# Gate and token transposes moved behind the next logits, tanh ahead of the normalisation, and beta's additions in half-size pieces

## The reference

```python
x = x + _L0_conv_ref(_gn(x), ...)     # temporal and spatial attention, graph convolution, layer norm
x = x + _L1_conv_ref(_gn(x), ...)     # mixture of experts: 8 experts, the best 2 for each position
```

```python
lhs = jnp.einsum('bnft,n->btf', x, U1) @ U2
rhs = jnp.einsum('f,bnft->bnt', U3, x)
E = jnp.einsum('kj,bij->bik', V_e, jax.nn.sigmoid(jnp.einsum('btn,bns->bts', lhs, rhs) + b_e))
x_tat = jnp.einsum('bnfj,bjt->bnft', x, _col_softmax(E))
lhs2 = jnp.einsum('bnft,t->bnf', x_tat, W1) @ W2
rhs2 = jnp.einsum('f,bnft->btn', W3, x_tat)
S = jnp.einsum('kj,bij->bik', V_s, jax.nn.sigmoid(jnp.einsum('bnt,btm->bnm', lhs2, rhs2) + b_s))
S = _col_softmax(S)
for k in range(3):
    r = jnp.einsum('mn,bmn,bmft->bnft', cheb[k], S, x)
    out = out + jnp.einsum('bnft,fo->bnot', r, Theta[k])
y = relu(rw * x + rb + conv_1x3(relu(out)) + tb)
return (y - mean(y)) / sqrt(var(y) + 1e-5) * gamma + beta      # over the last axis, 16 long
```

## Time and profile before

| what | us |
|---|---|
| median of 3 runs | 689.44 (686.73 to 690.37) |
| the profiled execution | 687.6 |
| its span | 685.8 |
| TensorE busy | 538.0 (78%) |
| VectorE busy | 395.7 (58%) |
| ScalarE busy | 253.8 (37%) |
| GpSimd busy | 198.6 (29%) |

### The profile page before, as it was taken

One profiled execution on the slowest core, in us unless ns is written; L12 is line 12 of the kernel. 1 busy time (PEld: TensorE's weight loads), 2 busy tenths in 40 slices (PEclk: granted clock), 3 DMA queues, 4 the chain that ended last, 5 costly groups with the idle time before them and its releaser, 6 DMA issues.

```text
span 685.8 us, 11952 instructions
## 1 busy us (share of the span) xinstructions
PE 538.0 (78%) x2664; PEld 363.6 (53%) x2665; DVE 395.7 (58%) x1697; ACT 253.8 (37%) x619; POOL 198.6 (29%) x267
## 2 busy tenths in 40 slices
PE   0557279989999999999983309999999999999243
PEld 0223147767776677676762204666666666665122
DVE  4745123788888888888899652333333333332265
ACT  0435833443444444444432201333333333333232
POOL 5000000113333333333334430434433433434000
PEclk9989558999999999999996557999999999999555
DMA  9900000000000000000010141222222222221697
GB/s 304 423 7 2 0 1 0 1 1 25 32 34 30 32 32 32 32 34 30 32 39 32 39 132 55 85 78 88 84 83 87 84 84 90 84 84 35 206 298 231
DMA packets 36260, 52.86 MB, mean 77 GB/s; under 512 B 4605, under 2 KB 31360, under 8 KB 35968
## 3 DMA queue, kind: packets, MB, share of 16 engines
q1 hardware_dynamic: 24816, 30.86, 14.3%
q0 software_dynamic: 6480, 16.85, 6.6%
q10 hardware_dynamic: 4928, 4.72, 2.1%
HBM read 30.19 MB, written 23.14 MB: 78 GB/s over the span
## 4 chain that ended last, share of the span: by engine, by line
PE 47%; DVE 31%; DMA 8%; issue 7%; ACT 4%; SPq 1%; POOL 1%; DVEq 0%; POOLq 0%; ACTq 0%
PE bank L614 18%; PE bank L629 9%; DMA xT<-yrows 5%; DVE vq L1012 4%; PE bank L492 4%; PE bank L601 2%; PE bank L622 2%; DVE vq L1011 2%; PE bank L377 2%; DVE work L1173 2%; PE bank L459 2%; DVE work L1189 2%; ACT xs L714 2%; DVE work L1224 1%; PE bank L367 1%
## 5 line engine op out<-in xcount | busy, mean ns | idle before, releaser
L614 PE MATMUL bank<-w,xT 128*128 x284 | 137.5, 607 | 2.0 <-DVE xT L1413 2.0
L1413 DVE COPY xT<-bank 128x256 f32<-128x256 f32 x71 | 30.2, 425 | 145.8 <-PE bank L601 145.8
L978 POOL DMA_INDIRECT yrows<-xT,dest x71 | 69.6, 980 | 141.1 <-ACT xT L834 137.0
L492 PE MATMUL bank<-work 128*128 128x256 f32 x384 | 95.0, 391 | 0.0
L946 POOL DMA_INDIRECT xrows<-xtok,slot x64 | 67.2, 1050 | 92.2 <-DVEq L1310 75.1
L492 PEld LDWEIGHTS bank<-work 128*128 128x128 f32 x384 | 71.9, 194 | 9.6 <-issue 0.8
L629 PE MATMUL bank<-w,xT 128*128 x284 | 73.3, 380 | 1.6 <-ACT xT L839 1.6
L935 POOL TENSOR_TENSOR yg<-work,sml 128x512 f32<-128x512 f32 x16 | 17.9, 1121 | 191.2 <-DVE work L1224 191.2
L614 PEld LDWEIGHTS bank<-w,xT 128*128 128x128 f32 x284 | 49.4, 194 | 38.1 <-issue 38.1
L828 ACT ACTIVATE xT<-bank 128x256 f32<-128x256 f32 x71 | 27.3, 384 | 97.4 <-PE bank L614 97.4
L629 PEld LDWEIGHTS bank<-w,xT 128*128 128x128 f32 x284 | 48.5, 190 | 6.2 <-issue 2.6
(11 more groups left out here) (200 smaller groups left out, 993.2 us busy)
## 6 DMA issues: line engine op xcount, KB each, us to landing
xT<-xrows SPq DMA_DIRECT2D x71, 129.0 KB
xT<-yrows SPq DMA_DIRECT2D x32, 256.0 KB, 3.9
xs<-x_in SPq DMA_DIRECT2D x4, 1024.0 KB, 10.2
w<-w13t_in SPq DMA_DIRECT2D x1, 4096.0 KB, 18.4
out<-xT ACTq DMA_DIRECT2D x16, 256.0 KB, 4.1
w<-w2t_in SPq DMA_DIRECT2D x1, 2048.0 KB, 22.8
yrows<-xT,dest POOLq DMA_INDIRECT x71, 2.4
xrows<-xtok,slot POOLq DMA_INDIRECT x64
```

Of the source, the lines that this page charges most:

```text
L492: last = mm(bank[6][:, h * N:(h + 1) * N], z[:, p, c, k, h], A[:, p, c, k], start=(c == 0 and k == 0), stop=(c == C - 1 and k == K - 1))
L614: last = mm(bank[2 + q][:, :], xc[:, q, c], w13[:, e, c].rearrange("p w n -> p (w n)"), start=(c == 0), stop=(c == C - 1))
L978: pool.indirect_dma_start(yrows, bass.IndirectOffsetOnAxis(ap=dest[:, q], axis=0), yo[:, q], None, bounds_check=2 * TOKENS - 1, oob_is_err ...
L1413: V.tensor_copy(xc[:, q].rearrange("p c k -> p (c k)"), bank[q][:, 0:C * P]).then_inc(c_xc, 1)
```

## The change

There are three edits. In the turn of the middle stage TensorE does `tokens` and `turn_logits` of an image one turn later, behind the logits and around the first part of the graph; ScalarE copies them at the start of that turn. ScalarE does `tanh` and the second `copy_features` ahead of `normalise`. On VectorE `route_a` is no longer woven with the statistics; it begins the chain that `route_b` continues. In the first stage `add_beta` takes a group: 16 pieces of 128x256 for each of the two, group 0's two by two behind the copies of group 1's images, and group 1's as 7, 1 and 8 around the second tanh and exp.

```diff
             def turn(i, q, ahead2, ahead1, now, back1, back2, back3):      # TensorE
                 if ahead1:
                     logits(i + 1, 1 - q)
+                if back3:
+                    tokens(i - 3, 1 - q)
                 if now:
                     graph(i, q, 0, 0)
+                if back3:
+                    turn_logits(i - 3, 1 - q)
+                if now:
                     graph(i, q, 0, 1)
...
                 if back3:
                     prefix(i - 3, 1 - q)
-                if back2:
-                    tokens(i - 2, q)
-                if back2:
-                    turn_logits(i - 2, q)
...
                     if j >= 2:
                         copy_x(g, j - 2)
+                    if g and j < GB:
+                        add_beta(0, 2 * j, 2 * j + 2)
...
-            def add_beta(first, end):
+            def add_beta(g, first, end):
 
-                act.wait_ge(a_xnv, B)
-                act.wait_ge(a_xna, B)
+                act.wait_ge(a_xnv, GB * (g + 1))
+                act.wait_ge(a_xna, GB * (g + 1))
                 for t in range(first, end):
-                    nc.scalar.activation(x_all[:, :, :, t], x_all[:, :, :, t], ACT.Identity,
+                    nc.scalar.activation(x_all[:, g, :, :, t], x_all[:, g, :, :, t], ACT.Identity,
...
-            add_beta(0, T // 2)
+            add_beta(1, 0, 7)
             temporal_tanh(1)
-            add_beta(T // 2, 3 * T // 4)
+            add_beta(1, 7, 8)
             temporal_exp(1)
-            add_beta(3 * T // 4, T)
+            add_beta(1, 8, T)
...
             def turn(i, q, ahead2, ahead1, now, back1, back2, back3):      # ScalarE
+                if back3:
+                    copy_tokens(i - 3, 1 - q)
                 if back1:
                     square(i - 1, 1 - q)
...
-                if back2:
-                    normalise(i - 2, q)
                 if ahead2:
                     tanh(i + 2, q)
                 if ahead1:
                     copy_features(i + 1, 1 - q, 1)
                 if back2:
-                    copy_tokens(i - 2, q)
+                    normalise(i - 2, q)
...
-            pool.wait_ge(x_beta, T)
+            pool.wait_ge(x_beta, GROUPS * T)
...
-                choice = router(route_b)
+                def choose():
+                    yield from router(route_a)
+                    yield from router(route_b)
+
+                choice = choose()
                 weave(centre())
-                weave(router(route_a), statistics())
+                weave(statistics())
                 variance = layer_norm()
                 weave(attention(), along=(variance, choice))
```

2 lines of the change are left out of this document (1 added, 1 removed).

## The result

| | median | range |
|---|---|---|
| kernel before, 4 runs | 688.53 us | 686.73 to 690.37 |
| changed kernel, 4 runs | 680.14 us | 677.81 to 684.61 |

The ratio is 0.9888 (95% interval 0.9853 to 0.9923): 7.7 us faster by the ratio, 8.4 by the medians. So the gain is some 8 to 10 us, with intervals of 2 us on either side. Among all the executions three were far slower than the rest (703 and 789 us of the kernel before, 1143 us of r2) and are left out. I had forecast 685.4, 4.0 us of gain, in a range from 681.2. The gain is about double, and the time outside the range.

A forecast was written before the change was run, and what follows sets the result against it. VectorE was taken to bound the middle stage, so removed TensorE or ScalarE waits count only where VectorE waits behind them. Gains of 2.0 + 1.7 + 0.3 + 0 = 4.0 us off 689.4 gave 685.4, range 681.2 to 690.5.

The forecast's parts named there:

- 682.9: Rival, chance 0.20: clock holds in the first stage and beta's pieces are at their lower bound, 2.5 us more gained.
- part 2: Router's first part on VectorE in steady turns: 0.18 us a turn, between 0.17 lost and 0.19 won.
- part 4: Last turns of the middle stage: 0.3 us gained once, bounds 0 and 3 x 0.31.
- three signs of being wrong: Steady turn not shorter, second exp moved by over 2.5 us, or square starting later behind L1198 than before.
- TensorE's waits: Gate and token transposes in steady turns: nothing gained, 0; bounds 0 and one 0.59 us copy a turn.
- The router's order: VectorE in eleven steady turns: 0.19 us won to the reciprocal, 0.01 lost behind it, 0.18 a turn, 2.0 in all.
- First turn with a router: Everything on TensorE comes 1.73 us earlier there: 1.7 us gained, bounds 0.58 and 1.73.
- The last turns: Statistics 0.31 us shorter, but tail the same chain as before: 0.3 us gained once.
- Beta: First stage: half pieces of 0.60 us on ScalarE, 1.5 us gained against 1.4 lost; 0 taken, bounds 2.5 gained, 2.3 lost.
- the clock was lost there: First stage: longer waits likely put TensorE's second eight transposes at 1.2 GHz, 1.4 us lost with the spreading matmuls.

The follow-up runs named there:

- r2: Kernel before with only beta's additions changed (half pieces, by group): 685.79 us, ratio 0.9968.
- r12: Changed kernel with ScalarE's normalisation put back ahead of tanh and the second feature copy: 688.81 us, ratio 1.0004 to the kernel before.
- r4: Kernel before with only VectorE's order changed (router's first part in one chain with the second, statistics alone): 686.12 us, ratio 0.9968.
- r6: Kernel before with only TensorE's and ScalarE's new turn orders; VectorE's order and beta as before: 686.46 us, ratio 0.9987.
- r3: Kernel before with only the three new turn orders (TensorE, ScalarE, VectorE), beta as before: 680.60 us, ratio 0.9902.
- filled pair: r13 and r15, kernel before and turns alone, both with result-neutral filler products on TensorE: 684.06 and 676.88 us.
- r13: Kernel before plus TensorE filler products that change no result, 8 at the pipeline's start and 31 ahead of the expert stage: 684.06 us, ratio 0.9948.
- r15: Kernel before with the three new turn orders only, plus the same fillers as r13: 676.88 us, ratio 0.9841.
- r1: The changed kernel unedited, run again beside the kernel before: 678.44 us, ratio 0.9849.
- r16: The whole changed kernel plus the same fillers as r13: 674.17 us, ratio 0.9817 to the kernel before.
- r14: Kernel before with beta's change only, plus the same fillers as r13: 682.01 us, ratio 0.9925.
- r17: r16 with 12 of group 0's beta pieces moved into ScalarE's wait for group 1's norm, four singly behind images 4 to 7: 669.09 us, ratio 0.9725.
- r19: r13 with 3 more fillers in front of the first image's tokens: 682.41 us, ratio 0.9916 to the kernel before.
- r7: Changed kernel with 24 filler products behind the last prefix product, ahead of the expert stage: 679.73 us, ratio 0.9865 to the kernel before.
- r9: Changed kernel with 29 filler products behind the last prefix product and 2 more ahead of the first expert product: 677.38 us, ratio 0.9832.

## Why the prediction was wrong

The time was forecast at 685.4 and came at 680.14. Of this distance 0.9 us is not the change's: I took the gain off 689.4, and the kernel before had 688.53 in the comparison. The rest is the gain, 4.0 forecast and 7.7 measured (8.4 by the medians). The range's lower end does not follow from its own terms either: 682.9 less 0.1 (part 2) and 0.6 (part 4) is 682.2, not 681.2; the upper end comes out at 690.7, not 690.5. None of the three signs of being wrong that I had named came (the steady turn is shorter, the second exp moved by 0.6 us, the square starts 0.78 behind L1198 where it was 0.79). None of them looked at the ends of the pipeline. By the parts of the sum:

1. **TensorE's waits, 0.** Right for the changed kernel: the square waits for VectorE and not for the token copy. What I did not see is how near the other side was. I argued that nothing on TensorE ahead of the copy waits any more; r12 shows that this hangs on tanh's new place, and what it is worth: 9 us.
2. **The router's order, 2.0.** Measured 2.15 in eleven turns, and L1198 to L1158 at 1.87, as said. The net of 0.18 a turn hid two small errors: 0.27 won ahead of the reciprocal (forecast 0.19) and 0.09 lost behind it (forecast 0.01). The router's steps there are ten now and seven before, not eight and five as I had counted; the three more are right. But the gain isn't VectorE's order alone (r4 makes the turn longer): it needs TensorE's and ScalarE's with it.
3. **First turn with a router, 1.7.** Measured 1.58, but I had put it all down to TensorE being 1.73 us earlier. With TensorE's and ScalarE's orders alone (r6) the turn is only 0.46 us shorter; the rest needs the router's first instruction out of the way on VectorE.
4. **The last turns, 0.3.** The step that failed. Measured 1.56 from last root to last prefix and 0.19 in the two turns ahead, 1.75 in all, above its bound of 0.93. I took the steady turn's 0.31 as the whole effect, and did not read the tail, where the router's first instruction waits 1.59 us in front of ready statistics.
5. **Beta, 0.** This is the larger shortfall, though within its bounds: timed alone beta brings 2.2 us (interval 1.0 to 3.4), near the favourable bound of 2.5, where I had taken the middle. The piece was right (0.62 to 0.64, forecast 0.60). From the same start (the changed kernel's first norm of group 1 starts 2.40 us later) the tanh of group 0 is at 55.39 - 2.40 = 53.0, as said, the first exp at 60.0 (forecast 59.0), and the second at 77.5 (forecast 76.0). It ends at 77.8, as it did before. The second eight transposes take 1.97 us, where it was 1.02: the clock was lost there, as feared. So in this profile the chain gained nothing up to there, as forecast; the timed gain stands somewhere else.

To this comes TensorE's clock in the old turns, which the sum had nowhere.

The terms found in the rows, 1.58 + 2.15 + 1.75 = 5.5, and 0.3 for the clock in the old turns, make 5.8; the turns' part timed 6.7 (r3). In the filled pair the rows of r13 and r15 give 3.28 for the first turn with a router (the fall included), 2.10, 0.42 and 1.54, in all 7.3, and it timed 7.4. Both times have intervals of 2 us on either side. With beta's 2.2 the sum without fillers is 8.0, against the 7.7 of the result and the 10.4 of r1.

**What stays open** is where beta's gain comes from. Between profiles in which the first stage went alike (r2 and before, both with group 0's products at 33.3 us from the first statistics) the first mix is 0.7 us earlier. Over the profiles without fillers ahead of it, the first mix comes 74.7 us behind the first statistics in seven with the new pieces (73.9 to 75.6) and 75.5 in five with the old ones (74.3 to 76.5), on average 0.8 earlier, with a scatter as large as that. In the filled pairs the clock at the pipeline's start rose near 86 us with the new beta and near 97 with the old one. r15, then r16:

```profile
70.00:75.00 5.00, 0.55 (x16) 0.47 (x16) 1.39 (x3) 5.00 (x6) 0.00 (x0) 0.86 0.00 0
...
85.00:90.00 5.00, 4.17 (x11) 2.16 (x10) 0.91 (x4) 1.29 (x3) 0.00 (x0) 0.50 0.00 0
```
```profile
70.00:75.00 5.00, 4.15 (x13) 1.98 (x12) 1.46 (x3) 3.24 (x6) 0.00 (x0) 0.78 0.01 2
...
85.00:90.00 5.00, 3.59 (x13) 1.90 (x12) 0.69 (x1) 1.35 (x3) 0.00 (x0) 0.91 0.01 3
```

TensorE works between 70 and 75 us with the new beta, where with the old it waits for ScalarE's full pieces, and in the filled kernels first mix to first root took 34.4 to 34.7 us with new beta (r14, r16, r17) and 37.8 with old (r13, r15, r19). That is 3.2 us in profiled runs, more than the timed 1.6. Without fillers ahead of the pipeline the same distance is 40.3 us six times and 37.8 twice with new beta, 42.0 twice, 40.3 twice and 37.8 once with old, on average 0.8 us apart. So a gain by the clock is seen beside the 0.7 to 0.8 of the first stage, and the two averages together would make the 1.6 to 2.2 us timed. But the profiles scatter by more than that, and no run holds the one fixed while the other moves, so this split is not shown.

## What to carry to other kernels

Read the first and the last turns of a software pipeline for themselves: an order that costs nothing in the steady turn (a wait long fulfilled) can put ready work behind a real wait where the pipeline fills (1.88 us in r6) and drains (1.59 us before). Time the edits of a change apart: here VectorE's order alone lengthened the steady turn that it shortens together with TensorE's. Where a change moves work to the head of an in-order queue, ask which other edit keeps its input early, and price the case without it. And where TensorE waits in every turn, the wait's price is its length and, in some executions, a spell at 1.2 GHz behind it.

## What the runs showed of the hardware

- The granted clock differs between executions of one kernel at the same place. The same expert stage took 220.4 to 220.8 us in six profiles without fillers ahead of it and 222.3 to 222.7 in six others, with its first products at 1.2 GHz for longer; with the clock held it took 218.7 to 219.4 in seven.
- Filler products that ended before the awaited work came gained nothing in that stage (r7, 222.8 us); with those that reached up to it the stage was 2 to 4 us shorter (r9).
- Half-size strided additions (256 elements a partition, 64 bytes apart) cost ScalarE 0.62 to 0.64 us, full ones (512) 1.04 to 1.14, so halves cost a tenth to a fifth more in all.
